# Layer 1 of a graph network on one core: six-row tiles, and three bf16 one-hots made by one VectorE instruction on 32-bit words

## The chip, the cores and the metric

The kernel runs on one core of a Trainium2 chip. The metric is the device time of one execution in microseconds (us); of several runs the median is taken. The engines are named as in the profile: PE is TensorE (PEld its weight loads), DVE is VectorE, ACT is ScalarE, POOL is GpSimd, SP is SyncE.

## The reference

A residual graph network of two layers, followed by a mixture-of-experts feed-forward. The graph has 6250 nodes of 256 features and 206250 edges sorted by destination, 33 a node on average. Cut to what matters here:

```python
deg_out = segment_sum(edge_weight, src); deg_in = segment_sum(edge_weight, dst)
norm = edge_weight * rsqrt(deg_out[src] * deg_in[dst] + EPS)
def gcn(x, W, b):
    xt = x @ W
    return relu(segment_sum(xt[src] * norm[:, None], dst) + b)
x = x + gcn(gcn(layernorm(x), W6, b6), W7, b7) @ Wp + bp
x = x + top2_of_8_experts(layernorm(layernorm(x)))
```

The matmuls and sums are in float32, and the edge weights enter the sums with float32 accuracy.

## The kernel before, in words

A first stage computes the out-degrees and the node features `xp`, a [node, feature] table kept in SBUF and also written to DRAM. Layer 1 then sums, for each destination node, the weighted rows of its edges' sources. It does so in two ways side by side.

**Dense part.** The first 720 tiles of 128 edges are put through adjacency blocks. A tile's edges (one on each partition) end at a few neighbouring destination rows: at most `TW`, counted from the row of its first edge. A chunk is 30 tiles (`CT`), 24 chunks in all; a chunk's tiles span at most 128 destination rows. A source node is number `128 * hi + lo`. For each tile DVE makes a key one-hot `ohk` of `KEYS = 49 * TW` columns (which `hi`, which row of the window) and a one-hot of `lo` with 128 columns, weighted with the edge weight. The weight is kept as three bf16 parts that add up to the float32 value, so there are three weighted one-hots. PE multiplies the three with `ohk` in three bf16 products that accumulate in one PSUM bank (`build_tile`, L1921): a tile's block of the adjacency, [128 `lo`, 49 `hi` x `TW` rows]. DVE adds it into the chunk's adjacency `adj` (128 x 49 x `AWID`, with `AWID = 128 + TW`) at a column offset read from a register (`add_tile`, L1199). When the chunk is complete, PE multiplies its 49 blocks with `xp` in float32 (`apply_step`, L1929; the profile shows two records for each float32 product). Meanwhile the next chunk is built in the other of two `adj` buffers; ACT zeroes the applied buffer slice by slice behind PE (L1634), and SP stores each built chunk to DRAM, from where layer 2 loads it again.

**Gathered part.** The other 112 groups of eight tiles gather their source rows from the table in DRAM, by eight indirect DMAs a group on POOL (L874), four groups ahead at most. DVE makes a group's one-hot matrices (`next_matrix`, L1208 to L1219), and PE sums (`sums`, L1949, begun by L1946 in every second group). 96 of the groups are spread over the loop of the dense part, 16 follow in a tail together with the node pairs' projections; layer 2 starts when the last pair has been stored.

**Order.** The loop has 12 iterations of 60 slots, one tile a slot; all orders are written out by hand, engine by engine. In slot t DVE adds tile t (it waits for `built`), then makes the one-hots of tile t + 4 (`OH_RING = 4`). PE waits until tile t is added, multiplies tile t + 3 (three PSUM banks), and then does the slot's share of the previous chunk's apply product: two blocks or one in slots 3 to 28 of a chunk, none in slots 29, 0, 1 and 2. The first addition of a chunk waits until ACT has zeroed all slices of its buffer, the last of which follows the last apply product of slot 28. Every ten tiles DVE loads ten column offsets into registers (L1186). In the first iteration the groups stand at slots 18, 23 and so on to 53, later at 2, 9 and so on to 51.

The one-hots of a tile in the code before:

```python
dve.tensor_scalar(ohk[:, r], iota_key[:, 0:KEYS], key[:, t:t + 1], None, ALU.is_equal)   # L1175
low_one_hot(t + 1)                                                                       # L1170
dve.tensor_tensor(parts[:, r], ohl[:, t % 2].unsqueeze(1).broadcast_to([P, 3, P]),       # L1181
                  w3t[:, :, t:t + 1].broadcast_to([P, 3, P]), ALU.mult)
```

Should a tile need more than `TW` rows (or another bound on the data not hold), a flag computed at run time sends all engines to a slow path.

Of the kernel before, what the change touches and what calls it, by code (L numbers as in the profile page):

```python
# [6 lines left out]
BF16 = mybir.dt.bfloat16  # L7
I32 = mybir.dt.int32
U32 = mybir.dt.uint32
ALU = mybir.AluOpType  # L10
# [4 lines left out]
P = 128  # L15
TG = 8
TS = 1
TI = 2
# [4 lines left out]
OH_RING = 4  # L23
# [8 lines left out]
CHUNKS = 24  # L32
CT = 30
DT = CHUNKS * CT
TW = 7
LOOP_GROUPS = 96
STEP_FROM = 3
GROUP_AT = [7 * s + 2 for s in range(GPI)]
# [38 lines left out]
def gnn_moe_kernel(nc, A):  # L77
    x, src, dst, ew = A["x"], A["src"], A["dst"], A["edge_weight"]
    out = A["out"]
# [32 lines left out]
    with ExitStack() as ctx:  # L112
        def sb(name, shape, dt=F32):
            return ctx.enter_context(nc.sbuf_tensor(name, shape, dt))

        def sem(name):
            return ctx.enter_context(nc.semaphore(name))
# [36 lines left out]
        iota_f = sb("iota_f", [P, P])  # L154
        iota_b = sb("iota_b", [P, P], BF16)
# [26 lines left out]
        zero = sb("zero", [P, 1])  # L182
# [4 lines left out]

        GAT_W = RING * TG * ROW
        OHK_W = OH_RING * (KEYS + 1) // 2
        PART_W = OH_RING * 3 * P // 2  # L190
        CM_W = 2 * P
        OHL_W = 2 * P // 2
        OHG_W = TG * WIN // 2
        XP_W = XB_ALL * ROW
        A_W = 2 * XB_ALL * AWID
        DTX = DT
        SC_W = 5 * DTX
        arena = sb("arena", [P, GAT_W + OHK_W + PART_W + CM_W + OHL_W + OHG_W + XP_W + A_W + SC_W])
        o_ohk = GAT_W
        o_part = o_ohk + OHK_W  # L200
        o_cm = o_part + PART_W
        o_ohl = o_cm + CM_W
        o_ohg = o_ohl + OHL_W
        o_xp = o_ohg + OHG_W
        o_a = o_xp + XP_W
        o_sc = o_a + A_W

        def area(first, words):
            return arena[:, first:first + words]
# [4 lines left out]


        ohk = area(o_ohk, OHK_W).bitcast(BF16).rearrange("p (r n) -> p r n", r=OH_RING)[:, :, 0:KEYS]
        parts = area(o_part, PART_W).bitcast(BF16).rearrange("p (r i n) -> p r i n", r=OH_RING, i=3)
        ohl = area(o_ohl, OHL_W).bitcast(BF16).rearrange("p (a n) -> p a n", a=2)
        xp = area(o_xp, XP_W).rearrange("p (h n) -> p h n", h=XB_ALL)
        adj = area(o_a, A_W).rearrange("p (a h w) -> p a h w", a=2, h=XB_ALL)  # L220
        key = area(o_sc, DTX)
        lo_f = area(o_sc + DTX, DTX)
        unread = area(o_sc + 2 * DTX, E8)
        w3t = area(o_sc + 2 * DTX, 3 * DTX // 2).bitcast(BF16).rearrange("p (i t) -> p i t", i=3)


        HIST = DRING * DU
# [168 lines left out]
        f_norm, f_T, f_xT, f_mm, f_feat = (sem(n) for n in ("f_norm", "f_T", "f_xT", "f_mm", "f_feat"))  # L396
        table_in = sems("table_in", 2)

        onehot_made, low_made, built, added = (sem(n) for n in ("onehot_made", "low_made", "built", "added"))
        zeroed, chunk_stored = sem("zeroed"), sem("chunk_stored")  # L400
        applied, zcd_ready, zd_stored, zk_in = (
            sems(n, 2) for n in ("applied", "zcd_ready", "zd_stored", "zk_in"))
# [48 lines left out]
        def bc_mid(ap, n):  # L451
            return ap.unsqueeze(1).broadcast_to([P, n, ap.shape[-1]])

        def bc_in(ap, n):
            return ap.unsqueeze(2).broadcast_to([P, ap.shape[-1], n])
# [5 lines left out]
        def in_twos(ap):  # L461
            return ap.rearrange("p (k t) -> p k t", t=TI)
# [474 lines left out]
        def _(dve):  # L937
# [228 lines left out]
            dve.tensor_copy(row_f[:, :], row_f[:, :]).then_inc(late_used, 1)  # L1166


            def low_one_hot(t):
                dve.tensor_scalar(ohl[:, t % 2], iota_b[:, :], lo_f[:, t:t + 1], None, ALU.is_equal).then_inc(low_made, 1)  # L1170

            def tile_one_hots(t):

                r = t % OH_RING
                dve.tensor_scalar(ohk[:, r], iota_key[:, 0:KEYS], key[:, t:t + 1], None, ALU.is_equal)  # L1175
                if t + 1 < DT:
                    if t:
                        dve.wait_ge(onehot_made, t)
                    low_one_hot(t + 1)
                dve.wait_ge(low_made, t + 1)  # L1180
                dve.tensor_tensor(parts[:, r], ohl[:, t % 2].unsqueeze(1).broadcast_to([P, 3, P]),  # L1181
                                  w3t[:, :, t:t + 1].broadcast_to([P, 3, P]), ALU.mult).then_inc(onehot_made, 1)

            def tile_offsets(t):

# [333 lines left out]
            with dve.If(bad < 1):  # L1519
                dve.wait_ge(scalars_made, 1)  # L1520
                next_matrix(0, 0)
                low_one_hot(0)
                for t in range(OH_RING):
                    tile_one_hots(t)
                for it in range(LOOP_GROUPS // GPI):
                    for u in range(2 * CT):
                        t = it * 2 * CT + u
                        if t % LOADED == 0:
                            offs = tile_offsets(t)
                        add_tile(t, offs[t % LOADED])  # L1530
                        if t + OH_RING < DT:
                            tile_one_hots(t + OH_RING)
                        if u in group_at(it):
                            n = it * GPI + group_at(it).index(u) + 1
                            next_matrix(0, n)

                def merge_rows(L):
                    dve.wait_ge(applied[L], SLICES * CHUNKS)
                    dve.wait_ge(zk_in[L], 16)
                    dve.wait_ge(zd_stored[L], 16 * (CHUNKS - 2))  # L1540
                    dve.tensor_tensor(zcd[:, (CHUNKS - 1) % 2], ps_ap, zk[:, :], ALU.add).then_inc(zcd_ready[L], 1)

                def tail_pair(b):
                    scale_pair(0, b, b, b % 2, b // 2, b - 1 if b > 1 else None, True)

                for k in range(TAIL):
                    if k == TAIL_FROM:
                        merge_rows(0)
                    n = LOOP_GROUPS + k + 1
                    if n < L1_GROUPS:  # L1550
                        next_matrix(0, n)
                    for b in TAIL_PAIRS[k]:
                        tail_pair(b)
                for b in range(LATE_PAIR, NPAIR):
                    tail_pair(b)
                next_matrix(1, 0)
                layer2_slots(layer2_slot)
                dve.wait_ge(seg_done, 2 * L1_GROUPS)
# [40 lines left out]
        def _(act):  # L1599
# [181 lines left out]
            def scalars():  # L1781

                act.activation(unread, w_sb[:, :], ACT.Relu, scale=-1.0, accum_out=bad_f[:, 4:5]).then_inc(act_checked, 1)
                act.wait_ge(act_checked, 1)
                act.activation(unread, w_sb[:, :], ACT.Relu, scale=1.0 / HUGE_EW, bias=minus_one[:, 0:1],
                               accum_out=bad_f[:, 5:6]).then_inc(act_checked, 1)
                act.wait_ge(act_checked, 2)
                act.copy(lo_f, src_lo[:, 0:DT])
                act.wait_ge(part_made, 3)
                act.copy(w3t.rearrange("p i (k t) -> p i k t", t=TI), w3[:, :, 0:DT // TI]).then_inc(scalars_made, 1)  # L1790

            def degree_iteration(it, load, pairs):
                for s in range(DUNITS):
# [93 lines left out]
        def _(pe):  # L1887
# [29 lines left out]
            def build_tile(t):  # L1917

                pe.wait_ge(onehot_made, t + 1)
                for i in range(3):  # L1920
                    last = pe.matmul(ps_b[t % len(ps_b)], parts[:, t % OH_RING, i], ohk[:, t % OH_RING], start=(i == 0),  # L1921
                                     stop=(i == 2))
                last.then_inc(built, 1)

            def apply_step(L, c, step):
# [380 lines left out]
```

## Time and profile before

| | us |
|---|---|
| device time, median of 3 runs (3751.34 to 3762.22) | 3759.06 |
| span of the profiled execution, first to last instruction | 3340.5 |
| median less span | 418.6 |
| PE busy | 2712.6 (81%) |
| DVE busy | 2059.8 (62%) |
| POOL busy | 2042.4 (61%) |
| ACT busy | 844.6 (25%) |

The profile is of one execution; its own device time is not listed, only its span. Busy time is an average over stages: until about 370 us the first stage, then layer 1 with its loop to about 1474 us and its tail to about 1664 us, then layer 2 and the experts. A busy PE is one with a matmul in flight, and POOL's busy time is that of issuing gathers.

### The profile page before, as it was taken

To read this page: it belongs to the slowest core of one execution; us is meant where nothing else is said; L and a number is where in the kernel's file an instruction comes from. 1 tells how busy PE (TensorE), PEld (TensorE's weight loads), DVE (VectorE), ACT (ScalarE), POOL (GpSimd) and SP (SyncE) were. 2 spreads that over 40 slices of the span, in tenths; PEclk is the share of its full clock that TensorE was granted. 3 is DMA by queue.
4 is the path that set the end of the run, shared out by engine and by line. 5 is a ranking of instruction groups with operands and counts; after the bars stand their busy time and mean duration, and the time that the engine had idled before them with its cause. 6 is when DMAs were issued, how large, how long until landed. Compare 5 with 4: busy or idle time off the path is not lost. (4 is left out here: it accounts for less than half of the span.)

```text
span 3340.5 us, 53436 instructions
## 1 busy us (share of the span) xinstructions
PE 2712.6 (81%) x17013; PEld 1994.4 (60%) x17013; DVE 2059.8 (62%) x6562; ACT 844.6 (25%) x1997; POOL 2042.4 (61%) x2012
## 2 busy tenths in 40 slices
PE   4567489999999999995577898899988845899984
PEld 3456156666666666663455666566666622789984
DVE  9999889999999999962201354455534556532210
ACT  5677511111111111102200110011100000456652
POOL 0000377777766766677277777777777755467753
PEclk8799699999999999998888999899999955899998
DMA  4010466655555555568456677677776564344434
GB/s 122 0 31 31 133 191 191 191 173 170 183 182 181 179 156 171 182 197 265 117 153 200 216 224 221 212 221 222 225 248 194 174 205 113 64 69 71 71 62 109
DMA packets 198560, 527.83 MB, mean 158 GB/s; under 512 B 40428, under 2 KB 128260, under 8 KB 192036
## 3 DMA queue, kind: packets, MB, share of 16 engines
q0 software_dynamic: 106176, 263.88, 31.7%
q1 hardware_dynamic: 89540, 245.64, 20.5%
q10 hardware_dynamic: 2592, 15.16, 1.1%
q8 instruction: 131, 2.15, 0.3%
q14 instruction: 121, 0.99, 0.1%
HBM read 380.37 MB, written 150.56 MB: 159 GB/s over the span
## 5 line engine op out<-in xcount | busy, mean ns | idle before, releaser
L874 POOL DMA_INDIRECT arena<-table,src_i x1792 | 1753.1, 978 | 699.0 <-issue 532.2
L1929 PE MATMUL bank<-arena 128*128 128x257 f32 x4704 | 1178.1, 387 | 2.4 <-ACT zcd L1643 2.4
L1929 PEld LDWEIGHTS bank<-arena 128*128 128x128 f32 x4704 | 868.4, 193 | 182.1 <-issue 61.8
L1921 PE MATMUL bank<-arena 128*128 128x343 bf16 x2160 | 450.8, 319 | 121.2 <-DVE arena L1199 89.0
L1199 DVE TENSOR_TENSOR arena<-arena,bank 128x343 f32 x720 | 363.9, 505 | 93.5 <-ACT arena L1634 45.2
L1181 DVE TENSOR_TENSOR arena<-arena 128x384 bf16<-128x384 bf16 x720 | 396.7, 551 | 0.0
L1921 PEld LDWEIGHTS bank<-arena 128*128 128x128 bf16 x2160 | 192.7, 98 | 334.8 <-DVE arena L1199 173.2
L1949 PE MATMUL bank<-arena,s_all 128*32 128x257 f32 x3584 | 317.7, 423 | 21.8 <-DMA arena<-table,src_i 21.8
L1624 ACT COPY zs<-bank 128x257 f32<-128x257 f32 x112 | 42.0, 375 | 947.8 <-PE bank L1949 947.8
L898 POOL DMA_INDIRECT acc<-arena x105 | 181.5, 1729 | 150.2 <-ACT arena L1749 125.9
L1451 DVE COPY arena<-arena 128x1024 f32 x105 | 75.6, 728 | 265.5 <-PE bank L2127 243.5
L1893 PE MATMUL bank<-arena 128*128 128x150 bf16 x1616 | 149.1, 252 | 111.1 <-DVE arena L1030 81.3
L1175 DVE TENSOR_SCALAR arena<-iota_key,arena 128x343 bf16<-128x343 bf16 x720 | 224.7, 312 | 0.0
L865 POOL PARTITION_ALL_REDUCE bad_all<-bad_f x1 | 0.4, 380 | 357.3 <-DVE bad_f L1163 357.3
L2136 PE MATMUL bank<-arena 128*128 x840 | 201.4, 383 | 15.2 <-ACT arena L1749 15.0
L1634 ACT COPY arena<-zero 128x2160 f32<-128x2160 f32 (+1 forms) x96 | 150.0, 1570 | 244.5 <-PE bank L1929 240.2
L2127 PE MATMUL bank<-arena 128*128 128x128 f32 x1680 | 210.9, 280 | 0.0
L1893 PEld LDWEIGHTS bank<-arena 128*128 128x128 bf16 x1616 | 129.5, 108 | 132.3 <-DVE arena L1030 112.7
L1949 PEld LDWEIGHTS bank<-arena,s_all 128*32 128x32 f32 x3584 | 128.2, 117 | 129.2 <-issue 58.8
L2127 PEld LDWEIGHTS bank<-arena 128*128 128x128 f32 x1680 | 202.3, 197 | 0.1
L1170 DVE TENSOR_SCALAR arena<-iota_b,arena 128x128 bf16<-128x128 bf16 x720 | 188.0, 261 | 0.0
L2136 PEld LDWEIGHTS bank<-arena 128*128 128x128 f32 x840 | 152.4, 192 | 35.2 <-issue 18.9
(239 smaller groups left out, 2911.4 us busy)
## 6 DMA issues: line engine op xcount, KB each, us to landing
chunks<-arena SPq DMA_DIRECT2D x24, 3307.5 KB
arena<-chunks SPq DMA_DIRECT2D x22, 3307.5 KB, 13.6
arena<-table,src_i POOLq DMA_INDIRECT x1792
zsum<-zc SPq DMA_DIRECT2D x112, 128.5 KB, 2.9
zrow<-zsum SPq DMA_DIRECT2D x50, 257.0 KB, 4.3
arena<-in_W ACTq DMA_DIRECT2D x16, 512.0 KB, 16.9
arena<-chunks ACTq DMA_DIRECT2D x2, 3307.5 KB, 16.4
rows_x<-arena SPq DMA_DIRECT2D x25, 264.0 KB, 4.4
```

What stands on the lines that cost most here:

```text
L874: pool.indirect_dma_start(gat[:, r, j, :], None, table[L], bass.IndirectOffsetOnAxis(ap=src_i[:, col:col + 1], axis=0)).then_inc(gathered[ ...
L898: pool.indirect_dma_start(acc, bass.IndirectOffsetOnAxis(ap=row_e[:, j:j + 1], axis=0), ye[:, j % 2], None, compute_op=ALU.add).then_inc(y ...
L1170: dve.tensor_scalar(ohl[:, t % 2], iota_b[:, :], lo_f[:, t:t + 1], None, ALU.is_equal).then_inc(low_made, 1)
L1175: dve.tensor_scalar(ohk[:, r], iota_key[:, 0:KEYS], key[:, t:t + 1], None, ALU.is_equal)
L1181: dve.tensor_tensor(parts[:, r], ohl[:, t % 2].unsqueeze(1).broadcast_to([P, 3, P]), w3t[:, :, t:t + 1].broadcast_to([P, 3, P]), ALU.mult) ...
L1199: dve.tensor_tensor(win, win, ps_b[t % len(ps_b)].rearrange("p (h w) -> p h w", w=TW), ALU.add).then_inc(added, 1)
L1893: last = pe.matmul(ps_do, oh_lo[:, r, j // TI, :, j % TI], whi[:, r, j // TI, :, :, j % TI].rearrange("p i n -> p (i n)"), start=False, st ...
L1921: last = pe.matmul(ps_b[t % len(ps_b)], parts[:, t % OH_RING, i], ohk[:, t % OH_RING], start=(i == 0), stop=(i == 2))
L1929: last = pe.matmul(ps_ap, adj[:, c % 2, h, 0:P], xp[:, h], start=(h == 0), stop=(h == XB_ALL - 1))
L1949: last = pe.matmul(ps_seg[q * WIN:(q + 1) * WIN, :], s_mat[:, r, q * HQ + j], gat[:, r, q * HQ + j], start=(j == 0 and not second), stop=( ...
L2127: last = pe.matmul(ps_h[j % 2][:, c], w1_e[:, j % W1_RING, k, c * P:(c + 1) * P], xeT[:, j % 2, k], start=(k == 0), stop=(k == KD - 1))
L2136: last = pe.matmul(ps_y, hs[:, j % 2, c], w2_of(e, c), start=(c == 0), stop=(c == HC - 1))
```

## The change

`TW` goes from 7 to 6, so `KEYS` goes from 343 to 294 and `AWID` from 135 to 134. The three weighted one-hots are no longer made from a bf16 one-hot of `lo` by a bf16 multiplication over 3 x 128. Instead, the three bf16 parts of a weight are laid into two 32-bit words (parts 1 and 0 as low and high half of the first, part 2 as high half of the second, whose low half is zero), and one float32 instruction compares `iota` with `lo` and multiplies the result, one or zero, with the two words: 2 x 128 words. A product with one leaves the bits of a word as they are. PE reads the halves that it needs from the words with a step of two bf16 elements. The separate `ohl` buffer, its semaphore `low_made` and DVE's wait on `onehot_made` go. ACT writes the halves and the zeros once (four copies instead of one).

```diff
-TW = 7
+TW = 6
...
-        PART_W = OH_RING * 3 * P // 2
+        PART_W = OH_RING * 2 * P
...
-        parts = area(o_part, PART_W).bitcast(BF16).rearrange("p (r i n) -> p r i n", r=OH_RING, i=3)
-        ohl = area(o_ohl, OHL_W).bitcast(BF16).rearrange("p (a n) -> p a n", a=2)
+        words = area(o_part, PART_W).rearrange("p (r i n) -> p r i n", r=OH_RING, i=2)
+        halves = area(o_part, PART_W).bitcast(BF16).rearrange("p (r i n h) -> p r i n h", r=OH_RING, i=2, h=2)
+        parts = [(0, 1), (0, 0), (1, 1)]
...
-            def low_one_hot(t):
-                dve.tensor_scalar(ohl[:, t % 2], iota_b[:, :], lo_f[:, t:t + 1], None, ALU.is_equal).then_inc(low_made, 1)
-
             def tile_one_hots(t):
 
                 r = t % OH_RING
                 dve.tensor_scalar(ohk[:, r], iota_key[:, 0:KEYS], key[:, t:t + 1], None, ALU.is_equal)
-                if t + 1 < DT:
-                    if t:
-                        dve.wait_ge(onehot_made, t)
-                    low_one_hot(t + 1)
-                dve.wait_ge(low_made, t + 1)
-                dve.tensor_tensor(parts[:, r], ohl[:, t % 2].unsqueeze(1).broadcast_to([P, 3, P]),
-                                  w3t[:, :, t:t + 1].broadcast_to([P, 3, P]), ALU.mult).then_inc(onehot_made, 1)
+                dve.scalar_tensor_tensor(out=words[:, r], in0=bc_mid(iota_f[:, :], 2), scalar=lo_f[:, t:t + 1],
+                                         in1=bc_in(w_words[:, t], P), op0=ALU.is_equal, op1=ALU.mult
+                                         ).then_inc(onehot_made, 1)
...
-                act.copy(w3t.rearrange("p i (k t) -> p i k t", t=TI), w3[:, :, 0:DT // TI]).then_inc(scalars_made, 1)
+                for i, (word, half) in enumerate(parts):
+                    act.copy(in_twos(w_halves[:, :, word, half]), w3[:, i, 0:DT // TI])
+                act.copy(w_halves[:, :, 1, 0], zero[:, :].broadcast_to([P, DT])).then_inc(scalars_made, 1)
...
-                for i in range(3):
-                    last = pe.matmul(ps_b[t % len(ps_b)], parts[:, t % OH_RING, i], ohk[:, t % OH_RING], start=(i == 0),
-                                     stop=(i == 2))
+                for i, (word, half) in enumerate(parts):
+                    last = pe.matmul(ps_b[t % len(ps_b)], halves[:, t % OH_RING, word, :, half], ohk[:, t % OH_RING],
+                                     start=(i == 0), stop=(i == 2))
```

On DVE, two tiles in the middle of the loop read as follows before (`iota_key` makes the key one-hot, `iota_b` the one-hot of `lo`, 128x384 the weighting, 128x49x7 the addition; ISA is the wait and register step of the addition):

```order
L1199 TENSOR_TENSOR arena<-arena,bank5 128x49x7
L1175 TENSOR_SCALAR arena<-iota_key,arena 128x343
L1170 TENSOR_SCALAR arena<-iota_b,arena 128x128
L1181 TENSOR_TENSOR arena<-arena 128x384
L1199 ISA
L1199 TENSOR_TENSOR arena<-arena,bank3 128x49x7
```

and so now, with the line numbers of the changed kernel:

```order
L1192 TENSOR_TENSOR arena<-arena,bank5 128x49x6
L1172 TENSOR_SCALAR arena<-iota_key,arena 128x294
L1173 SCALAR_TENSOR_TENSOR arena<-iota_f,arena 128x256
L1192 ISA
L1192 TENSOR_TENSOR arena<-arena,bank3 128x49x6
```

Four instructions with data a tile have become three; their order within a tile has not changed.

On PE, some slots of the loop before (the x3 are the products of a tile, into banks 3 to 5; bank 2 is the apply product, bank 0 the sums of a gathered group):

```order
L1921 MATMUL bank5<-arena 128x343 x3
L1929 MATMUL bank2<-arena 128x257 x2
L1946 MATMUL bank0<-zc,csel 1x257
L1949 MATMUL bank0<-arena,s_all 32x257 x8
L1921 MATMUL bank3<-arena 128x343 x3
```

and the same place now:

```order
L1915 MATMUL bank5<-arena 128x294 x3
L1923 MATMUL bank2<-arena 128x257 x2
L1940 MATMUL bank0<-zc,csel 1x257
L1943 MATMUL bank0<-arena,s_all 32x257 x8
L1915 MATMUL bank3<-arena 128x294 x3
```

PE's order is unchanged; only the products of a tile are narrower.

## Rows read from the trace of the kernel before

**Rows 1.** Head of the page: the span.

```profile
span 3340.5 us, 53436 instructions
```

**Rows 2.** The additions, L1199: duration min/median/max in ns, first and last start.

```profile
L1199 DVE TENSOR_TENSOR arena<-arena,bank x720: 495/505/522, 377.4 to 1473.9; 128x343 f32 x180
```

**Rows 3.** Busy time of each engine in a stretch of two chunks.

```profile
core 0: us, PE busy (x) PEld busy (x) DVE busy (x) ACT busy (x) POOL busy (x), PEclk, DMA share, GB/s
...
460.00:552.00 92.00, 84.40 (x539) 57.40 (x539) 83.46 (x260) 15.79 (x18) 70.67 (x71) 1.00 0.59 183
```

**Rows 4.** Waits of DVE and PE over the loop: us in total, times, longest.

```profile
DVE arena L1199 <- ACT arena L1634: 45.2, 23, 3.0
DVE arena L1199 <- issue: 28.0, 13, 3.9
DVE arena L1199 <- PE bank L1921: 18.4, 19, 1.3
...
PE bank L1921 <- DVE arena L1199: 89.0, 141, 4.6
```

**Rows 5.** Timeline of one tile in mid-chunk: start, duration (us), engine, line.

```profile
906.49 0.50 DVE L1199 TENSOR_TENSOR arena<-arena,bank 128x343 f32 x1
906.91 0.30 DVE L1175 TENSOR_SCALAR arena<-iota_key,arena 128x343 bf16<-128x343 bf16 x1
...
907.12 0.60 PE L1921 MATMUL bank<-arena 128*128 128x343 bf16 x3
907.13 0.28 DVE L1170 TENSOR_SCALAR arena<-iota_b,arena 128x128 bf16<-128x128 bf16 x1
907.29 0.55 DVE L1181 TENSOR_TENSOR arena<-arena 128x384 bf16<-128x384 bf16 x1
...
907.56 1.03 PE L1929 MATMUL bank<-arena 128*128 128x257 f32 x4
...
907.76 0.50 DVE L1199 TENSOR_TENSOR arena<-arena,bank 128x343 f32 x1
...
908.43 0.60 PE L1921 MATMUL bank<-arena 128*128 128x343 bf16 x3
```

**Rows 6.** Timeline around a chunk's end; in brackets the idle time before and what ended it.

```profile
971.85 0.60 PE L1921 MATMUL bank<-arena 128*128 128x343 bf16 x3
972.05 0.64 ACT L1634 COPY arena<-zero 128x540 f32<-128x540 f32 x1 [0.68 <-PE bank L1929]
...
972.83 0.51 DVE L1199 TENSOR_TENSOR arena<-arena,bank 128x343 f32 x1 [1.90 <-ACT arena L1634]
...
973.40 0.61 PE L1921 MATMUL bank<-arena 128*128 128x343 bf16 x3 [0.95 <-DVE arena L1199]
...
978.97 1.07 PE L1929 MATMUL bank<-arena 128*128 128x257 f32 x2
```

**Rows 7.** The gathers of layer 1, what they waited for, and who waited.

```profile
L874 POOL DMA_INDIRECT arena<-table,src_i x896: 940/948/1459, 376.5 to 1602.2; - x180
...
  PE bank L1949: 68.8, 32
...
  PE bank L1946: 0.8, 1
```

**Rows 8.** Groups of DVE before the loop, by form: busy us, mean ns, idle.

```profile
L1133 DVE SCALAR_TENSOR_TENSOR arena<-arena 128x416 f32<-128x416 f32 x1 | 0.9, 907 | 0.0
...
L1133 DVE SCALAR_TENSOR_TENSOR arena<-arena 128x720 f32<-128x720 f32 x1 | 0.9, 903 | 0.0
...
L1133 DVE SCALAR_TENSOR_TENSOR arena<-arena 128x1 f32<-128x1 f32 x2 | 0.2, 152 | 0.0
```

**Rows 9.** Weight loads of three lines: duration min/median/max in ns.

```profile
L1893 PEld LDWEIGHTS bank<-arena x1616: 95/98/150, 21.7 to 340.8; 128*128 128x128 bf16 x180
...
L1921 PEld LDWEIGHTS bank<-arena x2160: 94/97/153, 373.5 to 1473.2; 128*128 128x128 bf16 x197
...
L1929 PEld LDWEIGHTS bank<-arena x4704: 185/190/339, 428.4 to 2665.5; 128*128 128x128 f32 x196
```

**Rows 10.** Timeline of PE: start of the sums of group 7.

```profile
462.54 0.38 PE L1946 MATMUL bank<-zc,csel 128*1 128x257 f32 x1
```

More of the change, by code:

```diff
@@ L189, in gnn_moe_kernel @@
         OHK_W = OH_RING * (KEYS + 1) // 2
-        PART_W = OH_RING * 3 * P // 2
+        PART_W = OH_RING * 2 * P
         CM_W = 2 * P
-        OHL_W = 2 * P // 2
         OHG_W = TG * WIN // 2
@@ L197, in gnn_moe_kernel @@
         SC_W = 5 * DTX
-        arena = sb("arena", [P, GAT_W + OHK_W + PART_W + CM_W + OHL_W + OHG_W + XP_W + A_W + SC_W])
+        arena = sb("arena", [P, GAT_W + OHK_W + PART_W + CM_W + OHG_W + XP_W + A_W + SC_W])
         o_ohk = GAT_W
@@ L201, in gnn_moe_kernel @@
         o_cm = o_part + PART_W
-        o_ohl = o_cm + CM_W
-        o_ohg = o_ohl + OHL_W
+        o_ohg = o_cm + CM_W
         o_xp = o_ohg + OHG_W
@@ L223, in gnn_moe_kernel @@
         unread = area(o_sc + 2 * DTX, E8)
-        w3t = area(o_sc + 2 * DTX, 3 * DTX // 2).bitcast(BF16).rearrange("p (i t) -> p i t", i=3)
+        w_words = area(o_sc + 2 * DTX, 2 * DTX).rearrange("p (t i) -> p t i", i=2)
+        w_halves = area(o_sc + 2 * DTX, 2 * DTX).bitcast(BF16).rearrange("p (t i h) -> p t i h", i=2, h=2)
         HIST = DRING * DU
@@ L397, in gnn_moe_kernel @@
         table_in = sems("table_in", 2)
-        onehot_made, low_made, built, added = (sem(n) for n in ("onehot_made", "low_made", "built", "added"))
+        onehot_made, built, added = (sem(n) for n in ("onehot_made", "built", "added"))
         zeroed, chunk_stored = sem("zeroed"), sem("chunk_stored")
@@ L1521, in _ @@
                 next_matrix(0, 0)
-                low_one_hot(0)
                 for t in range(OH_RING):
```

## The prediction

> **What bounds the kernel now.** I read the span first [rows 1]: 3340.5 us from the first to the last instruction. The three timed runs have a median of 3759.06 us, so 418.6 us of a run lie around the span; the profiled execution's own time is not listed, and I take those 418.6 us as unchanged and make the sum on the span. The change touches one stage, the dense part of layer 1. Its 720 additions run from 377.4 to 1473.9 us [rows 2], 1096.5 us for 24 chunks of 30 tiles, 45.7 us a chunk. In a stretch of two chunks (92 us) both PE (84.4) and DVE (83.5) are busy nine tenths, at a full PE clock [rows 3]. Busy shares cannot rank two engines that wait for each other, so I went to the waits: over the loop PE waits 89.0 us for DVE's addition, and DVE waits 45.2 us for ACT's zeroing and only 18.4 us for a product of PE [rows 4]. Then the pace of one tile [rows 5]. On DVE, start to start: addition 0.42 us (906.49 to 906.91), key one-hot 0.22, low one-hot 0.16, weighting 0.47, together 1.27. On PE: the three products of a tile 0.44 (907.12 to 907.56), two blocks of the apply product 0.87, together 1.31. So in the 26 of 30 slots that carry apply work PE is a little slower than DVE, and in the other four, around a chunk's end, PE has nothing but products and DVE sets the pace. Such an end reads so [rows 6]: the last apply is over at 971.85, ACT zeroes the last slice at 972.05, DVE adds at 972.83, PE goes on at 973.40, and the next apply begins only at 978.97: 7.1 us.
>
> A third engine is close behind: POOL issues the gathers. 896 of them start between 376.5 and 1602.2 us, of which it waits 68.8 us for PE to free a buffer, so unhindered one takes (1602.2 + 0.9 - 376.5 - 68.8) / 896 = 1.29 us, a group of eight 10.3 us. PE waited for a gather once, 0.8 us [rows 7].
>
> **The change, part by part.**
> *DVE.* The two one-hot steps, low (0.16) and weighting (0.47), become one scalar_tensor_tensor over 256 32-bit elements with two float32 sources. Nearest rows: the same operation over 720 takes 903 ns and over one 152 ns [rows 8], so (903 - 152) / 719 = 1.04 ns an element and 152 + 255 x 1.04 = 0.42 us for 256. Each DVE row in [rows 5] is followed 0.08 us before its end, so it adds 0.34 us. Upper bound: the row over 416 elements, whose sources are read every fourth word, takes 907 ns, 1.82 ns an element: 0.62 us busy, 0.54 added. I take 0.34, because the new sources are a run and a repeated element as in the 720 row. The key one-hot has 49 elements fewer; 215 fewer save 0.06 us (L1175 against L1170), so 49 save 0.01: 0.21. The slots of its ring now start 590 bytes apart, every second one on a half word, and no row shows such a store; the upper bound for those is one element each 1.04 ns, 0.38 us, or 0.09 more per tile on average. I take none. The Trainium skill ("VectorE: DVE Perf Modes", Mode 2x_1P) asks for a 4-byte aligned start for packed 16-bit work, which would give that upper bound and 3 x 0.09 x 22 = 6 us less gain; no run here shows it yet. The addition loses 49 x 1.04 = 0.05: 0.37. A tile goes from 1.27 to 0.37 + 0.21 + 0.34 = 0.92 us of DVE.
>
> *PE.* Three products of 294 columns instead of 343: 0.44 x 294 / 343 = 0.38, 0.06 less per tile. The weights are read with a step of two. The out-degree products of the first stage already do this: their loads take 95 ns at least and 98 in the median, against 94 and 97 for this stage's contiguous ones [rows 9]. A load of 98 ns fits under a product of 0.38 / 3 = 0.126 us, so I cost the step at nothing; the cover is that product, and it is gone above 126 ns.
>
> *The rest.* ACT makes four small copies once instead of one, in the degree stage where DVE is the busy engine; chunk rows have 134 words in place of 135. Both at nothing. Whether six rows are enough is a matter of data: in the reference's input 151 of the 720 tiles span four rows, 512 five, 57 six and none seven, so the slow path isn't taken.
>
> *The sum.* In the 26 apply slots DVE (0.92) no longer keeps pace with anything: PE at 0.38 + 0.87 = 1.25 sets it, and a chunk gains what PE gains there, 26 x 0.06 = 1.6 us. So a third of a microsecond saved on DVE per tile is worth little in these slots. At the chunk's end DVE paces three steps, from the addition at 972.83 to the one that releases the next apply: 3 x 0.35 = 1.05, and the first addition and last product are 0.05 and 0.06 shorter: 1.15 us. What is late next there is ACT's zeroing, which stays. Together 2.8 us a chunk, 45.7 to 42.9. The first two chunks gain nothing: the gathers of group 7 are issued at 376.5 + 8 x 10.3 = 459 us and land some 2 us on, and its sums, in slot 53 of 60, now start at 462.54 [rows 10], so POOL holds that point. From there 22 chunks remain: 22 x 2.8 = 62 us. Then POOL needs 8 x 10.3 = 82.7 us for two chunks and PE 85.8, so POOL stays ahead, barely. Behind the loop the tail and layer 2 hang on the loop's last apply and move with it whole. Span 3340.5 - 62 = 3278.5; time 3759 - 62 = **3697 us**.
>
> **Rivals.**
> *The new instruction runs at half speed.* Two float32 sources at the strided row's 1.82 ns an element add 0.54: the DVE tile is 1.12, still under PE's 1.25. Only the chunk's end changes, 3 x 0.15 + 0.11 = 0.56 instead of 1.15: 22 x 2.2 = 48 us, **3711**. For it: the 416 row. Against it: the 720 row, also two float32 sources in SBUF, at 1.04 ns. The Trainium skill ("Vector Engine (DVE) Microarchitecture Reference", Points that are easy to get wrong) states that this operation with two SBUF sources that aren't bf16 loses half its throughput; the trace's 720 row disagrees. Chance 0.13.
> *POOL becomes the bound.* DVE then touches SBUF with two 32-bit sources on every tile, and gathers may stretch: single ones go up to 1459 ns where the median is 948 [rows 7]. The loop is POOL's once a gather takes 85.8 / 64 = 1.34 us instead of 1.29, and all gain is gone at 91.4 / 64 = 1.43. Half way, 1.385, two chunks take 88.6 us: 11 x 2.8 = 31 us gained, **3728**. Even unstretched, POOL limits an upside: it has 69 us of waits to give back, and beyond them PE would wait. Chance 0.10.
> *More than forecast.* DVE's stalls that PE now shares (28.0 us of "issue" at register loads [rows 4]) vanish behind a DVE that runs ahead: up to 25 us more, held by POOL to about 88 in all: **3675**. Chance 0.10.
> *Slower.* The loads of half words, place L1921, cost what this kernel's 32-bit loads cost, 190 ns in the median [rows 9]: above 0.126 they pace PE, three loads 0.57 against 0.44 now, +0.13 x 26 = 3.4 us a chunk; less the 1.15 at the chunk's end it is 2.2 x 22 = 48 us slower, **3807**. It turns into a loss where 26 x 3 x (load - 0.147) exceeds 1.15, at 0.162 us a load. Against it: the strided loads at 98 ns. Chance 0.06.
> *No change.* The DVE tile stays at 1.27, 0.35 above my sum; both upper bounds together give 0.29 more on the tiles that have both, so it takes something that no row shows. **3759**. Chance 0.06.
>
> **How the numbers follow.** The forecast, PE pacing the loop, gets 0.55, with a range of its own from 3684 to 3711. The range of 8 in 10 reaches to the half-speed and POOL cases above and the fuller gain below: 3672 to 3735. About 0.3%, 11 us, is what a measurement of this kernel tells from no change. Faster: forecast, half speed, POOL and more than forecast, 0.88, less 0.02 for a POOL stretched to its break-even and past it: 0.86. Same: no change and half of that 0.02: 0.07. Slower: the load case and the other half: 0.07.
>
> **What the profile after would show.** The new one-hot line at about 420 ns and gone L1170 and L1181; the addition at 455 ns; strided loads near 98 ns and products of 294 columns 0.126 us apart; PE's wait for DVE's addition down from 89 to some 50 us, and DVE's wait for PE's products up from 18 to well over 200 us, since DVE now runs ahead; the last addition at about 1412 us; POOL's wait for PE nearly gone. It would be wrong if DVE still paced the apply slots, if loads rose over 126 ns, or if PE's waits for gathers grew.

## The result, and the profile after

The changed kernel takes 3736.66 us (median of 5 runs, 3717.70 to 3737.58) against 3762.22 for the kernel before on the same chip. The ratio of the two is 0.9908, interval 0.9880 to 0.9936: faster by 24 to 45 us, about 35, where 62 were forecast. On the 3759.06 us that the forecast started from, the ratio gives 3724, 27 us above it. One of the twelve runs of e8 below took 5321.52 us, where its others took 3754.50 to 3791.23, and is in no ratio.

The first thing to read in the new profile is its head. The profiled execution took 3717.70 us and its span is 3715.9, so 1.8 us lie around the span, not 418.6. The execution shown of the kernel before [rows 1] was therefore one that ran some 11% faster than the runs that were timed; that has to be known to understand every number below. The next lines are from the page of the changed kernel, groups with count, busy us, mean ns, idle time before them and what ended it.

```profile
span 3715.9 us, 52719 instructions
...
L1192 DVE TENSOR_TENSOR arena<-arena,bank 128x294 f32 x720 | 328.6, 456 | 434.4 <-PE bank L1915 175.8
L1915 PEld LDWEIGHTS bank<-arena 128*128 128x128 bf16 x2160 | 200.1, 102 | 429.9 <-DVE arena L1192 154.3
...
L1173 DVE SCALAR_TENSOR_TENSOR arena<-iota_f,arena 128x256 f32<-128x256 f32 x720 | 341.6, 475 | 0.0
...
L1172 DVE TENSOR_SCALAR arena<-iota_key,arena 128x294 bf16<-128x294 bf16 x720 | 216.6, 301 | 0.0
```

The parts are nearly the size that was forecast: the addition 456 ns (455), the strided loads 102 (98), the new instruction 475 (420). Its tile on DVE, from the timeline:

```profile
904.76 0.29 DVE L1172 TENSOR_SCALAR arena<-iota_key,arena 128x294 bf16<-128x294 bf16 x1
904.97 0.48 DVE L1173 SCALAR_TENSOR_TENSOR arena<-iota_f,arena 128x256 f32<-128x256 f32 x1
905.37 0.46 DVE L1192 TENSOR_TENSOR arena<-arena,bank 128x294 f32 x1
905.74 0.29 DVE L1172 TENSOR_SCALAR arena<-iota_key,arena 128x294 bf16<-128x294 bf16 x1
```

Start to start that is 0.21 + 0.40 + 0.37 = 0.98 us against 1.27 [rows 5] and a forecast of 0.92. But the loop as a whole is not what the parts make (all additions, duration min/median/max, first and last start):

```profile
L1192 DVE TENSOR_TENSOR arena<-arena,bank x720: 441/455/466, 377.7 to 1611.3; 128x294 f32 x180
```

1233.6 us, more than the 1096.5 of [rows 2], although DVE's work on a tile and PE's products are shorter. The waits over the loop (us in total, times, longest) show stops of up to 7 us that [rows 4] do not have. "Remote" stands for a wait for which the trace shows no instruction that ended just before it was over, "issue" for one with nothing shown.

```profile
DVE arena L1192 <- PE bank L1915: 175.8, 120, 7.4
...
DVE arena L1192 <- remote: 135.6, 57, 7.4
POOL arena L874 <- remote: 113.9, 67, 4.7
POOL arena L874 <- PE bank L1943: 113.0, 26, 8.1
PE bank L1915 <- DVE arena L1192: 94.9, 35, 7.0
PE bank L1915 <- issue: 81.9, 66, 5.4
```

One such stop in the timeline, at the sums of a group:

```profile
874.15 1.21 PE L1943 MATMUL bank<-arena,s_all 128*32 128x257 f32 x13
...
875.29 0.55 PE L1915 MATMUL bank<-arena 128*128 128x294 bf16 x3
...
876.54 0.54 PE L1915 MATMUL bank<-arena 128*128 128x294 bf16 x3
...
877.79 0.54 PE L1915 MATMUL bank<-arena 128*128 128x294 bf16 x3
...
878.52 0.38 ACT L1616 COPY zs<-bank 128x257 f32<-128x257 f32 x1 [15.35 <-remote]
878.75 0.46 DVE L1192 TENSOR_TENSOR arena<-arena,bank 128x294 f32 x1 [2.67 <-PE bank L1915]
878.76 0.95 POOL L874 DMA_INDIRECT arena<-table,src_i  x1 [1.60 <-remote]
...
879.73 0.46 DVE L1192 TENSOR_TENSOR arena<-arena,bank 128x294 f32 x1
...
880.71 0.46 DVE L1192 TENSOR_TENSOR arena<-arena,bank 128x294 f32 x1
```

PE's products follow each other by 1.25 us, exactly the slot that was forecast (875.29, 876.54, 877.79). The sums are over at 875.4 and the first of these products at 875.8, yet ACT, DVE and POOL all go on only at 878.5 to 878.8, some 3 us late and together. They wait for two different signals of PE: ACT and POOL for that of the sums, DVE for that of a tile's products. DVE then takes the additions 0.98 us apart, faster than PE makes products, so these had long been there. What came late is PE's signals, not its work. The trace shows this directly, since it also records when a signal (a semaphore update) arrives. Those of the three products come at 878.55, 878.64 and 878.72, in one bunch, and the products' ends, which the profile models, are 875.84, 877.09 and 878.33. Of the 701 signals of PE that are recorded between 380 and 1380 us, 51% come over 0.5 us after the nearest earlier end of a matmul that gives this signal; of DVE's 923 and ACT's 91 none does, and none of PE's 867 in the trace of [rows 1]. At a chunk's end the same happens to the signal of the last apply, and there nothing else is left to do: in one such end ACT's zeroing starts at 913.93, 5.6 us after that apply is over at 908.32 (0.20 us in [rows 6], 971.85 to 972.05), PE stands still for 5.81 us, and in the 12 us around it, 910 to 922, the granted clock is 0.57: half of the 2.4 GHz for most of them. The last line is that stretch, with the columns of [rows 3].

```profile
907.29 1.03 PE L1923 MATMUL bank<-arena 128*128 128x257 f32 x4
...
913.93 0.64 ACT L1626 COPY arena<-zero 128x536 f32<-128x536 f32 x1 [1.30 <-remote]
...
915.23 1.89 PE L1915 MATMUL bank<-arena 128*128 128x294 bf16 x6 [5.81 <-DVE arena L1192]
...
910.00:922.00 12.00, 6.65 (x32) 2.39 (x32) 7.25 (x23) 2.55 (x3) 3.32 (x4) 0.57 0.65 255
```

### The profile page after: what moved, and what is told of

It is laid out like the page before. It is cut to its first block and busy times, and to the rows that moved or that the text cites. A ratio compares the mean times of both kernels' runs of the same rounds, so it can differ in the third digit from the quotient of the medians.

```text
span 3715.9 us, 52719 instructions
## 1 busy us (share of the span) xinstructions
PE 2808.8 (76%) x17013; PEld 2028.3 (55%) x17013; DVE 1852.4 (50%) x5842; ACT 848.4 (23%) x2000; POOL 2029.5 (55%) x2012
## 5 line engine op out<-in xcount | busy, mean ns | idle before, releaser
L1923 PE MATMUL bank<-arena 128*128 128x257 f32 x4704 | 1250.4, 401 | 97.8 <-ACT zcd L1635 52.1
L1923 PEld LDWEIGHTS bank<-arena 128*128 128x128 f32 x4704 | 893.0, 201 | 301.4 <-issue 172.8
L1915 PE MATMUL bank<-arena 128*128 128x294 bf16 x2160 | 431.1, 311 | 211.8 <-DVE arena L1192 94.9
L1192 DVE TENSOR_TENSOR arena<-arena,bank 128x294 f32 x720 | 328.6, 456 | 434.4 <-PE bank L1915 175.8
L1943 PE MATMUL bank<-arena,s_all 128*32 128x257 f32 x3584 | 333.3, 431 | 34.9 <-issue 20.5
L1173 DVE SCALAR_TENSOR_TENSOR arena<-iota_f,arena 128x256 f32<-128x256 f32 x720 | 341.6, 475 | 0.0
L1626 ACT COPY arena<-zero 128x2144 f32<-128x2144 f32 (+1 forms) x96 | 149.1, 1560 | 356.9 <-PE bank L1923 218.2
L1172 DVE TENSOR_SCALAR arena<-iota_key,arena 128x294 bf16<-128x294 bf16 x720 | 216.6, 301 | 0.0
L2121 PEld LDWEIGHTS bank<-arena 128*128 128x128 f32 x1680 | 202.1, 197 | 0.1
L2130 PEld LDWEIGHTS bank<-arena 128*128 128x128 f32 x840 | 151.7, 191 | 36.2 <-issue 18.8
L1955 PE MATMUL bank<-zs,arena 128*128 128x257 f32 x224 | 79.1, 437 | 91.6 <-issue 52.6
```

The costliest lines, as they stand in the source:

```text
L1173: dve.scalar_tensor_tensor(out=words[:, r], in0=bc_mid(iota_f[:, :], 2), scalar=lo_f[:, t:t + 1], in1=bc_in(w_words[:, t], P), op0=ALU.is_ ...
L1192: dve.tensor_tensor(win, win, ps_b[t % len(ps_b)].rearrange("p (h w) -> p h w", w=TW), ALU.add).then_inc(added, 1)
L1626: act.copy(adj[:, c % 2, first:last], zero[:, :].unsqueeze(2).broadcast_to([P, last - first, AWID])).then_inc(zeroed, 1)
L1915: last = pe.matmul(ps_b[t % len(ps_b)], halves[:, t % OH_RING, word, :, half], ohk[:, t % OH_RING], start=(i == 0), stop=(i == 2))
L1923: last = pe.matmul(ps_ap, adj[:, c % 2, h, 0:P], xp[:, h], start=(h == 0), stop=(h == XB_ALL - 1))
L1943: last = pe.matmul(ps_seg[q * WIN:(q + 1) * WIN, :], s_mat[:, r, q * HQ + j], gat[:, r, q * HQ + j], start=(j == 0 and not second), stop=( ...
```

## The experiments

Every ratio is to the kernel before on the same chip, with its 95% interval. "Loop" is the time from the first to the last addition in the run's profile, "clock" the mean granted clock from 600 to 1380 us.

| run | ratio | loop us | clock |
|---|---|---|---|
| changed kernel | 0.9908 (0.9880 to 0.9936) | 1233.6 | 0.94 |
| e1 before, again | one run, 3803.11 us | 1303.1 | 0.93 |
| e2 six rows alone | 0.9993 (0.9969 to 1.0018) | 1300.5 | 0.92 |
| e3 one instruction alone | 0.9880 (0.9849 to 0.9911) | 1264.9 | 0.94 |
| e4 even slots | 0.9885 (0.9852 to 0.9917) | 1259.3 | 0.93 |
| e5 one-element extra | 0.9917 (0.9888 to 0.9946) | 1244.1 | 0.93 |
| e6 slower key one-hot | 1.0003 (0.9977 to 1.0029) | 1275.3 | 0.91 |
| e7 shorter apply | 0.9916 (0.9889 to 0.9944) | 1248.7 | 0.91 |
| e8 two products | 1.0031 (1.0009 to 1.0054) | 1275.8 | 0.88 |
| e9 four banks | 0.9868 (0.9848 to 0.9888) | 1261.8 | 0.93 |
| e10 half the gathers | 0.8285 (0.8269 to 0.8302) | 1015.9 | 0.99 |
| e11 half the sums | 0.9964 (0.9947 to 0.9981) | 1247.9 | 0.91 |
| e12 no key one-hot | 0.9943 (0.9922 to 0.9964) | 1289.4 | 0.91 |

e1 to e4 ran on one chip, where the kernel before takes 3817.82 us; e5 to e8 on another (3764.45); e9 to e12 on a third (3816.48). The changed kernel's ratio was taken on none of these three, so a comparison with it goes by ratios across chips; on the first chip e4 stands in for it. "Loop" and "clock" are of one execution each.

**e1, the kernel before as it is.** No edit.

> The kernel before, unchanged, for a second profile. Theory A (the shown profile is what the timed runs were, and 418 us of a run lie around the span): its span is again about 3340 us with a time near 3759, and PE's waits for nothing shown (issue) at the products stay near nothing. Theory B (the shown execution was a faster one than the timed runs): span and time lie within some 2 us of each other, about 3755 us; the 720 additions take well over 1200 us instead of 1096.5; and PE shows stops of several us with no releaser, some 80 us at the products, as the changed kernel does (81.9).

Its time was 3803.11 us and its span 3801.3. Its additions, and one of its chunk ends:

```profile
L1199 DVE TENSOR_TENSOR arena<-arena,bank x720: 495/506/516, 377.2 to 1680.3; 128x343 f32 x180
```

```profile
887.60 1.03 PE L1929 MATMUL bank<-arena 128*128 128x257 f32 x4
...
891.87 0.64 ACT L1634 COPY arena<-zero 128x540 f32<-128x540 f32 x1 [3.89 <-remote]
...
892.65 0.51 DVE L1199 TENSOR_TENSOR arena<-arena,bank 128x343 f32 x1 [4.64 <-issue]
```

Theory B holds. The kernel before has the late signals too: the apply is over at 888.63 and ACT learns of it at 891.87. Its loop is 1303.1 us, 206.6 longer than in the execution of [rows 2], with the same instructions at the same durations. The stage ahead of the loop, which has no gathers, is the same to 0.2 us (377.2 against 377.4).

**e2, six rows a tile alone.**

```diff
-TW = 7
+TW = 6
```

> Six rows a tile alone, with the old low one-hot and weighting. Theory A (PE paces the apply slots, the forecast): PE gains 26 x 0.06 = 1.6 us a chunk and the chunk's end 0.3, 22 x 1.9 = 42 us faster than before, most of the gain. Rival B (stops of PE pace the loop and hide a part of it): half of that, about 20 us. Rival C (DVE paced the loop, and its 0.6 us of two one-hot steps were the cost): 0 to 15 us, as a DVE tile is only 0.06 us shorter.

Ratio 0.9993: the narrower products and additions bring nothing that can be measured, at most 12 us of the 42.

**e3, the one instruction alone.**

```diff
-TW = 6
+TW = 7
-        SC_W = 5 * DTX
+        SC_W = 5 * DTX - 64
```

(on the changed kernel; the second edit only makes room).

> The one instruction for the three parts alone, with seven rows a tile (343 columns). Theory A: PE's slots stay at 1.31 us, only the chunk's end gains 3 x 0.23 = 0.7 us (the instruction adds 0.40 us in the changed kernel against 0.63 for the two steps), 22 x 0.7 = 15 us. Rival B: the DVE that runs ahead takes no stop from PE, 0 to 15 us. Rival C (DVE paced the loop): over 25 us, the whole gain of the change.

Ratio 0.9880, 34 to 58 us faster: the whole gain of the change. On the one chip the loops are 1303.1 before, 1300.5 with six rows, 1264.9 with the instruction and 1259.3 with both (e4).

**e4, ring slots on whole words.**

```diff
-        OHK_W = OH_RING * (KEYS + 1) // 2
+        OHK_W = OH_RING * (KEYS + 2) // 2
```

> The changed kernel with one more spare column in a slot of the key one-hot's ring, so that every slot starts on a whole word (592 bytes apart instead of 590). If the start on a half word costs: the key one-hot's mean falls from 301 ns to about 275, a DVE tile from 0.97 to 0.93 us, and the time by 3 x 0.04 x 22 = 3 us at the chunks' ends, or up to 0.04 x 720 = 29 us if DVE paces the loop. If it costs nothing: 301 ns and the same time as the changed kernel.

The key one-hot has a mean of 297 ns instead of 301, and the ratio, 0.9885, does not differ from the changed kernel's:

```profile
L1172 DVE TENSOR_SCALAR arena<-iota_key,arena 128x294 bf16<-128x294 bf16 x720 | 214.2, 297 | 0.0
```

A start on a half word costs some 4 ns on average here, not the 90 of the upper bound.

**e5, one more small instruction.**

```diff
+        spare = sb("spare", [P, 8])
...
+                dve.memset(spare[:, t % 8:t % 8 + 1], 0.0)
```

> The changed kernel with one more VectorE instruction a tile, of one element (720 more, into a spare tile; about 0.07 us each). Theory D (the gain is DVE's shorter tile: after each late signal of PE, DVE works off the waiting additions at its own pace): 0.07 of the 0.30 us a tile is given back, a quarter of the gain, some 10 us. Rival N (the number of instructions and signals is what counts, since every engine's records and signals share a path that is late): nearly all of the 43 us is given back, as the number of VectorE instructions is again that of before.

0.9917: rival N falls as far as it is about the number of instructions. The signals that the change took away (`low_made`, 720 of them) were not put back, so their share stays untested. Theory D's quarter is neither shown nor excluded: an undisturbed tile takes 0.98 us with the extra instruction and 0.97 without, so that this run hardly lengthened it.

**e6, a slower key one-hot.**

```diff
-        iota_key = sb("iota_key", [P, KEYS + 1], BF16)
+        iota_key = sb("iota_key", [P, KEYS + 1])
```

> The changed kernel with the key one-hot's row of numbers kept as float32 instead of bf16, so that the same instruction takes some 0.2 us longer (294 elements at 1.04 ns in place of 0.30 busy), with no instruction more. Theory D: a DVE tile is about 1.2 us again, and most of the gain is gone: ratio to before 0.996 to 1.0. Rival N: the time stays at the changed kernel's ratio, 0.989.

```profile
L1172 DVE TENSOR_SCALAR arena<-iota_key,arena 128x294 bf16<-128x294 f32 x720 | 269.9, 375 | 0.0
```

The instruction became only 0.07 us longer, not 0.2, and the ratio is 1.0003: the whole gain is gone. By theory D a quarter should be. Set beside e3, whose tile is as long, this speaks against D. Two additions with nothing idle between them, in e3 and then in e6:

```profile
900.12 0.51 DVE L1192 TENSOR_TENSOR arena<-arena,bank 128x343 f32 x1
...
901.16 0.51 DVE L1192 TENSOR_TENSOR arena<-arena,bank 128x343 f32 x1
...
705.61 0.45 DVE L1192 TENSOR_TENSOR arena<-arena,bank 128x294 f32 x1
...
706.66 0.46 DVE L1192 TENSOR_TENSOR arena<-arena,bank 128x294 f32 x1
```

At 1.04 us a tile e3 has the whole gain, at 1.05 e6 has none. So the length of DVE's tile does not by itself decide.

**e7, a shorter apply.**

```diff
+                    n = ROW if L or h in (0, XB_ALL - 1) else 193
-                    last = pe.matmul(ps_ap, adj[:, c % 2, h, 0:P], xp[:, h], ...
+                    last = pe.matmul(ps_ap[:, 0:n], adj[:, c % 2, h, 0:P], xp[:, h, 0:n], ...
```

> The changed kernel with 193 of 257 columns in the apply products of layer 1 but the first and the last of each chunk (it leaves out a quarter of the apply sums). PE has 4 x 0.054 = 0.22 us less a slot, with as many instructions. Theory A (PE paces the apply slots, the forecast): 26 x 0.21 x 22 = 120 us faster than the changed kernel, until POOL (12 us a group) holds it at about 96 us for two chunks, 50 us. Theory D with late signals: PE is not what is waited for, below 20 us.

0.9916: 0.22 us less of PE's work in each apply slot brings nothing, at a clock of 0.91 instead of 0.94.

**e8, two products.**

```diff
-                for i, (word, half) in enumerate(parts):
+                for i, (word, half) in enumerate(parts[:2]):
...
-                                     start=(i == 0), stop=(i == 2))
+                                     start=(i == 0), stop=(i == 1))
```

> The changed kernel with two of the three products of a tile (it leaves out the third part of the weights). PE has 0.126 us and one load and one product less a slot. Theory A: 26 x 0.126 x 22 = 72 us faster than the changed kernel, less where POOL holds it. Rival N: PE's instructions fall by a ninth in the loop, so up to 100 us. Theory D: below 20 us, and like the shorter apply per microsecond of PE work saved.

1.0031: less work on PE made it slower than the changed kernel by over 1%. The stretch from 600 to 1380 us (busy us and instructions by engine, clock, DMA share, GB/s):

```profile
600.00:1380.00 780.00, 608.28 (x3466) 390.52 (x3465) 498.61 (x1496) 118.08 (x135) 478.56 (x478) 0.88 0.49 154
```

The same stretch of the changed kernel:

```profile
600.00:1380.00 780.00, 661.33 (x4058) 438.52 (x4058) 519.16 (x1553) 121.90 (x140) 493.79 (x496) 0.94 0.52 162
```

A clock of 0.88 instead of 0.94 means that 12% more of the time, some 94 us of these 780, is at 1.2 GHz.

**e9, four banks.**

```diff
-        ps_b = [bank[i][:, 0:KEYS] for i in (3, 4, 5)]
+        ps_b = [bank[i][:, 0:KEYS] for i in (3, 4, 5, 6)]
```

> The changed kernel with four banks instead of three between PE's products and DVE's additions. Theory D (signals of PE come 2 to 5 us late in the stages with gathers, and three tiles, 3 x 1.25 us, do not cover that): a fourth tile covers 1.25 us more of each of some ten stops in two chunks, as far as DVE's one-hot ring of four allows it, 11 x 5 = 50 us or less gained on the changed kernel (ratio 0.975 to 0.988). Theory A (PE paces by its own work): nothing, 0.989 to 0.991.

0.9868, the fastest that computes everything; its interval overlaps those of the changed kernel and of e4, so it is not shown to be better. It lies in theory D's range and outside A's, but both ranges start from the changed kernel's ratio on another chip.

**e10, half of the gathers.**

```diff
-                for j in range(TG):
+                for j in range(0, TG, 2):
...
-                pe.wait_ge(gathered[r], (m // RING) * (16 * TG) + 16 * TG)
+                pe.wait_ge(gathered[r], (m // RING) * (8 * TG) + 8 * TG)
```

> The changed kernel with every second gather of a group left out (it sums stale rows for the others). If the lateness of PE's signals hangs on the gathers that are under way, ACT's copy follows the last matmul of a group's sums after about 0.5 us as in the shown profile of before, instead of 3.5, and two chunks take some 92 us or less instead of 100.5. If it hangs on PE's own instructions, the copy stays at some 3 us and the two chunks at 98 to 101.

This run settles most. The edit holds for both layers, so the ratio has layer 2's gathers in it too; the loop alone goes from 1261.8 us (e9, on the same chip) to 1015.9. A group's sums in its timeline, with the same matmuls as in the changed kernel:

```profile
878.53 1.21 PE L1943 MATMUL bank<-arena,s_all 128*32 128x257 f32 x13
...
879.83 0.38 ACT L1616 COPY zs<-bank 128x257 f32<-128x257 f32 x1 [1.52 <-PE bank L1943]
880.06 1.13 POOL L874 DMA_INDIRECT arena<-table,src_i  x1 [5.01 <-PE bank L1943]
```

Its additions, and its stretch:

```profile
L1192 DVE TENSOR_TENSOR arena<-arena,bank x720: 446/459/474, 378.2 to 1394.1; 128x294 f32 x180
```

```profile
600.00:1380.00 780.00, 744.83 (x4843) 521.52 (x4842) 622.69 (x1850) 143.31 (x164) 287.96 (x296) 0.99 0.42 141
```

ACT's copy now starts 1.3 us after the 13 matmuls began; in the changed kernel it was 4.4 (874.15 to 878.52). The clock is 0.99, PE is busy 95% of the stretch, and two chunks take 1015.9 / 12 = 84.7 us. Of PE's signals 2% are over 0.5 us late, by the count that gave 51% above. The lateness hangs on the gathers. POOL's issuing and the DMA traffic (141 instead of 162 GB/s) fell with them, and which of these it is was not separated.

**e11, half of the sums.**

```diff
-                for j in range(HQ):
+                for j in range(1):
...
-                                         stop=(j == HQ - 1 and bool(second)))
+                                         stop=bool(second))
```

> The changed kernel with four of the eight sums of a group left out; the gathers are all issued. If the lateness hangs on the burst of short matmuls in a group's sums, it falls to about half (ACT's copy 1.5 to 2 us after the last one instead of 3.5) and two chunks take 5 us less or more. If it hangs on the gathers, it stays, and only some 0.7 us of PE a group goes, which counts for nothing.

With half as many matmuls in a group's sums and all gathers, two chunks take 1247.9 / 12 = 104.0 us (102.8 in the changed kernel), and the lateness stays: 2.9 us from the last sum's end to ACT's copy in the median, against 3.2. The sums' burst on PE is not the cause. The ratio, 0.9964, is worse than the changed kernel's, but not by the loop, which is 14 us shorter than e9's on the same chip; the edit holds for layer 2 as well, and in the profiled execution what was lost lies outside the loop.

**e12, no key one-hot after the first four tiles.**

```diff
+                if t < OH_RING:
-                dve.tensor_scalar(ohk[:, r], iota_key[:, 0:KEYS], key[:, t:t + 1], None, ALU.is_equal)
+                    dve.tensor_scalar(ohk[:, r], iota_key[:, 0:KEYS], key[:, t:t + 1], None, ALU.is_equal)
```

> The changed kernel without the key one-hot after the first four tiles (the products use stale ones). DVE's tile falls by another 0.21 us, from 0.97 to 0.76. Theory D, DVE's own pace between PE's late signals still counts: 0.21 of 0.30 us, some 25 to 30 us faster than the changed kernel (ratio about 0.982). If DVE is now short enough that PE's work and its late signals are all that is left: ratio 0.988 to 0.991.

0.9943: a DVE tile shorter by another 0.21 us is no gain. It is a loss against e9 on the same chip, and rather one against the changed kernel, though these two intervals overlap. Neither side of the expectation fits.

## Why the prediction was right in its sign, and why its size was off

**The step that failed** is the second sentence of the prediction: "418.6 us of a run lie around the span", taken as unchanged. They do not lie around the span (1.8 us do). They lie within it, 206.6 us of them in the loop (e1 against [rows 2]): stops, and a slower clock (0.93), that the execution shown did not have. Everything that was read from its waits [rows 4, 6] was true of that execution and not of those that were timed.

**PE sets the pace of the apply slots, and a chunk gains what PE gains there: 26 x 0.06 = 1.6 us.** This term was 22 x 1.6 = 35 of the 62 us; in the timed runs e2 shows nothing of it that can be measured, at most 12. The step itself was read rightly, since a slot of PE is 1.25 us where PE runs (875.29 to 876.54). But PE does not pace a loop in which others learn of its work 3 to 5 us late: three banks are 3 x 1.25 us of lead, which such a delay uses up (a fourth, in e9, was not shown to help). Narrower products (e2), a shorter apply (e7) and a product less (e8) were worth nothing or less.

**"A third of a microsecond saved on DVE per tile is worth little in these slots."** Here the sum was too low: e3 has the whole gain, 46 us, where its chunk ends would give 15 by the prediction's terms. Why is open. Theory D says: after a late signal several additions wait, and DVE works them off at its own pace while PE goes on at 1.25 to 1.31 us a slot; at 1.27 us a tile DVE hardly catches up, at 0.98 it does. That is argued, and the runs do not bear it out: e3 and e6 have the same tile and opposite outcomes, and in e12 a still shorter one brings nothing. What the runs show is that the one instruction in place of two steps carries the gain, not how.

**Where the rest of the gain goes.** Part of the answer is the clock. Where PE stands for 4 to 6 us, the granted clock is at half afterwards: 0.57 in the 12 us above, and under 0.75 in the next 5 us after each of the changed kernel's 17 stops of 4 us or more between 380 and 1400 us. e6, e7, e11 and e12 have 0.91 and e8 0.88 in the loop, where the changed kernel, e3 to e5 and e9 have 0.93 or 0.94. The three that left out work of PE alone (e7, e8, e11) are all among the lower. An estimate from these rows: 0.03 of the clock over a loop of 1275 us is 38 us of PE at full speed, about what e6 lost; but e7 has the same 0.91 and lost nothing, and the kernel before has 0.93 (e1), so the clock does not explain the gain itself. What decides in which kernel the stops meet PE so was not settled.

**What the forecast would have been worth.** In e10, without the lateness, two chunks take 84.7 us where the prediction had 85.8 for the changed kernel. Its picture of the loop is near when signals come in time, though with half of the gathers POOL could not be the bound there. The gain against a kernel before without the lateness was not measured.

**The smaller terms.** DVE's tile: 0.98 instead of 0.92, because the new instruction adds 0.40, not 0.34. By its mean it is 152 + 255 x 1.27 ns, between the 1.04 of the 720 row and the 1.82 of the strided row [rows 8]. The addition takes (505 - 455) / 49 = 1.02 ns an element. The rule of the Trainium skill ("Vector Engine (DVE) Microarchitecture Reference", Points that are easy to get wrong), half the throughput with two SBUF sources that are not bf16, would make the instruction 152 + 255 x 2.04 = 672 ns, an estimate from that rule and the addition's rate; the trace has 475 and disagrees. Key one-hot and addition were right to 0.01. The other rule, a 4-byte aligned start ("VectorE: DVE Perf Modes", Mode 2x_1P, in the Trainium skill), would have cost 6 us; e4 shows 4 ns an instruction and no time. Strided loads: 102 ns, under a product, as costed.

**The rivals and the signs.** Half speed and loads at 190 ns did not come. POOL is not the bound: its gathers take 974 ns in the mean (978 before), and its waits rose instead of vanishing, from 68.8 us [rows 7] to 113.0 + 113.9, because the signal that frees its buffers is among the late ones. So the outcome, 3724 by the ratio, is near the time of the POOL rival (3728), but not by its mechanism. That it lies within the forecast's 3672 to 3735 is in part luck: the 35 us of PE's slots did not come, and DVE's instruction brought more than its term. Of the signs, PE's wait for DVE's addition did not fall from 89.0 to some 50 us (it is 94.9), and the last addition starts at 1611.3 us, not at 1412.

## What to carry to other kernels

Before a trace is used for a sum, compare its span with the timed median: a gap of a tenth was, here, time within the span that this trace did not show, and its waits, its clock and its ranking of engines were not those of the timed runs. Where an engine's signals come late, as PE's do here, saved work on that engine can be worth little (e2, e7, e8); test each part of a change alone, since here one part held all of the gain and the other none. Of all edits halving the gathers moved the time most (e10), far more than any arithmetic left out.

## What the runs showed of the hardware that was not expected

Halving the number of indirect gathers took the kernel from 0.99 to 0.83 of the time before, although the engine that issues them waited for others. With all of them under way, signals of PE, and of PE alone among PE, DVE and ACT, reached ACT, DVE and POOL up to 5.6 us late and several at once; with half, 0.1 us after the last sum's modelled end (879.74 to 879.83). How gathers hold back another engine's signals stays open, and so does why one execution, that of [rows 1], was free of it with all gathers in place. One candidate that no run here tested: the Trainium skill ("NOTIFIC — the notification-queue block", Overflow: three behaviours, one of which stalls the engine) states that the block which writes the profiler's records can, in one of its settings, stall the engine that gives them when the memory for them is full. In the stop shown above PE's products went on every 1.25 us while its signals were late, so a stalled PE alone does not explain it.

Taking work from PE went with a lower granted clock: 0.94 with three products a tile, 0.88 with two (600 to 1380 us, one execution each).
